# Turning two context tiles per transpose in the first expert layer, with an f32 product for the spread maxima and one-step rounding in the ternary layer

## The reference

```python
x = x + tanh(g_xattn[0]) * L0_xattn(layernorm(x), ctx)
x = x + tanh(g_ffn[0])   * L0_ffn(layernorm(x))      # 64 experts, top 6 by groups, capacity 64, plus shared
x = x + tanh(g_xattn[1]) * L1_xattn(layernorm(x), ctx)
x = x + tanh(g_ffn[1])   * L1_ffn(layernorm(x))      # ternary weights, 8-bit rounded activations
x = x + tanh(g_xattn[2]) * L2_xattn(layernorm(x), ctx)
x = x + tanh(g_ffn[2])   * L2_ffn(layernorm(x))      # 16 experts
x = x + tanh(g_xattn[3]) * L3_xattn(layernorm(x), ctx)
x = x + tanh(g_ffn[3])   * L3_ffn(layernorm(x))      # 8 experts plus shared
```

```python
# L1..L3_xattn: the same rotated context is key and value
kv_rope = kv_c * cos + rotate_half(kv_c) * sin
scores  = einsum('bhsr,bhlr->bhsl', q_r, kv_rope @ W_kr)
attn    = softmax(scores)
# L1_ffn, before each of its three matmuls
s  = 127 / clip(max(abs(x), -1), 1e-5)
qx = clip(round(x * s), -128, 127) / s
```

## Time and profile before

| | |
|---|---|
| time, median of 3 runs | 2348.73 us (2344.44 to 2351.06) |
| the profiled execution's own time | 2347.95 us |
| its span, first to last instruction | 2345.6 us |
| PE busy | 2209.3 us, 94% of the span |
| DVE, POOL, ACT busy | 1542.6, 1391.7, 1064.5 us |
| granted TensorE clock, mean | 0.958 |
| chain that ended last, share of PE | 82% |

### The profile page before, as it was taken

The page is one execution under the profiler, slowest core; times in us unless marked ns, Lnnn a source line. Parts: engine busy times, 40 slices in busy tenths (PEclk is TensorE's granted clock), DMA queues, the critical chain, the costliest instruction groups (busy, mean ns, idle before and its releaser), DMA issues.

```text
span 2345.6 us, 31158 instructions
## 1 busy us (share of the span) xinstructions
PE 2209.3 (94%) x11484; PEld 1551.9 (66%) x11484; DVE 1542.6 (66%) x2502; ACT 1064.5 (45%) x1573; POOL 1391.7 (59%) x901
## 2 busy tenths in 40 slices
PE   7789999899999997798999999989998999999988
PEld 5578888765665655565556656567886666656587
DVE  6766652478878856765878877652334788788653
ACT  4453443554555544311455555443434545555443
POOL 0352210278888874366688888824443888888744
PEclk9898999999999998799899999998999999999989
DMA  3124655211111103100121121015531111111022
GB/s 90 48 62 138 196 161 160 82 40 40 54 47 40 41 16 125 42 1 11 50 60 40 40 59 41 7 46 148 151 105 54 40 40 58 42 40 46 6 63 75
DMA packets 55394, 152.76 MB, mean 65 GB/s; under 512 B 8453, under 2 KB 14421, under 8 KB 54860
## 3 DMA queue, kind: packets, MB, share of 16 engines
q1 hardware_dynamic: 54860, 150.44, 21.3%
q10 hardware_dynamic: 384, 0.33, 0.1%
HBM read 135.88 MB, written 14.86 MB: 64 GB/s over the span
## 4 chain that ended last, share of the span: by engine, by line
PE 82%; DVE 7%; POOL 3%; ACT 2%; DMA 2%; issue 2%; SPq 0%; POOLq 0%; ACTq 0%; DVEq 0%
PE psum L890 20%; PE psum L1365 19%; PE psum L1355 10%; PE psum L1336 10%; PE psum L1357 10%; PE psum L1521 2%; PE psum L1476 2%; PE psum L1382 2%; POOL CL L1808 1%; PE psum L1250 1%; PE psum L1544 1%; PE psum L1128 1%; DMA WqrT<-in_a_WrT 1%; DMA bd<-in_blockdiag 1%; DVE mx L2333 1%
## 5 line engine op out<-in xcount | busy, mean ns | idle before, releaser
L1786 ACT ACTIVATE E<-psum 125x896 f32<-125x896 f32 x576 | 528.3, 920 | 581.1 <-PE psum L1357 554.2
L2336 DVE TENSOR_REDUCE mx<-psum 128x1 f32<-128x500 f32 x945 | 611.8, 675 | 171.9 <-PE psum L1336 170.0
L2085 POOL TENSOR_TENSOR SA<-SA,E 125x896 f32<-125x896 f32 x282 | 597.1, 2117 | 22.1
L1365 PE MATMUL psum<-E,V 125*64 125x448 f32 x2304 | 472.2, 545 | 0.0
L1355 PE MATMUL psum<-Q,K 128*125 128x448 f32 x1152 | 331.5, 369 | 2.3 <-ACT E L1786 2.3
L1336 PE MATMUL psum<-K,Q 128*128 128x500 f32 x945 | 328.7, 402 | 3.1 <-DVE Q L2274 1.9
L1357 PE MATMUL psum<-Q,K 128*125 128x448 f32 x1152 | 329.8, 367 | 0.0
L1365 PEld LDWEIGHTS psum<-E,V 125*64 125x64 f32 x2304 | 152.9, 136 | 228.6 <-issue 223.3
L2085 POOL TENSOR_TENSOR SA<-SA,SB 125x896 f32<-125x896 f32 x93 | 194.3, 2089 | 153.6 <-DVE SB L2359 153.6
L1336 PEld LDWEIGHTS psum<-K,Q 128*128 128x128 f32 x945 | 174.2, 188 | 134.1 <-issue 33.1
L1355 PEld LDWEIGHTS psum<-Q,K 128*125 128x125 f32 x1152 | 213.2, 187 | 37.1 <-ACT E L1786 6.9
(11 more groups left out here) (303 smaller groups left out, 3712.8 us busy)
## 6 DMA issues: line engine op xcount, KB each, us to landing
K<-kt_scratch SPq DMA_DIRECT2D x48, 750.0 KB, 4.9
K<-kt_scratch SPq DMA_DIRECT2D x48, 375.0 KB, 6.0
EW<-in_f_w SPq DMA_DIRECT2D x64, 256.0 KB, 6.3
kt_scratch<-kt SPq DMA_DIRECT2D x16, 750.0 KB, 4.3
WS<-in_f_w SPq DMA_DIRECT2D x31, 384.0 KB, 4.8
GB<-gates_scratch SPq DMA_DIRECT2D x36, 224.0 KB, 3.7
WoT<-in_a_WoT SPq DMA_DIRECT2D x24, 256.0 KB, 3.1
V<-in_ctx SPq DMA_DIRECT2D x16, 375.0 KB
```

The costliest lines, as they stand in the source:

```text
L1365: i = e.matmul(psum[c * DC:(c + 1) * DC, 4 + b % 2, 0:HT], V[0:LP, b, k * DC:(k + 1) * DC], E[g[n, b, k] % NE][0:LP, half[c]], start=k == ...
L1786: e.activation(E[m % NE][0:LP, :].rearrange("p (c q) -> p c q", c=2), psum[0:LP, pair:pair + 2, 0:HT], ACT.Exp).then_inc(exp_set.sem, 1)
L2085: e.tensor_tensor(SA[b % 2][0:LP, :], a[0:LP, :], x[0:LP, :], ALU.add).then_inc(sum_set.sem, 1)
L2336: e.tensor_reduce(mx[:, b % 2, j * 3 + c:j * 3 + c + 1], psum[:, bank, 0:CW], AX.X, ALU.max).then_inc(small_free.sem, 1)
```

## The change

1. A `cturn` turns six tiles by three transposes of two neighbouring tiles each (125 x 128 into 128 x 125 of PSUM). In PSUM the even tiles then stand in partitions 0 to 63 and the odd ones in 64 to 127. ACT and DVE each take them out by two instructions of 64 x 3 x 125, one for the even and one for the odd tiles, which write every second block of 125 columns of `kt`. A batch has two `cturn`s in place of three, `cadd` stands a step earlier, and the last `cturn` of a batch stands a step earlier, so that `cstore` waits for `kl_set` of turn 1 in place of turn 2.
2. `nm` becomes an f32 tile, and the `max_spread` product takes `ident` (f32); `identr` and its copy go.
3. `quantise` is one instruction: the subtraction of ROUND moves into ACT's copy out of PSUM as an immediate bias, and the minimum with 127 is left out.

```diff
-        steps += [first + [("cturn", b, 0)], [], [("cturn", b, 1)], last, [("cturn", b, 2)]]
+        steps += [first + [("cturn", b, 0)], [], last, [("cturn", b, 1)], []]
...
-    nm = mem.take("nm", [P, 2, DC], F32R)
-    identr = mem.take("ident_r", [P, P], F32R)
+    nm = mem.take("nm", [P, 2, DC], F32)
...
+    def turned_keys(b, g, odd, row):
+
+        return kt[b % 2][row:row + DC, 6 * g * LP:6 * (g + 1) * LP].rearrange("p (j k l) -> p j k l", k=2, l=LP)[:, :, odd, :]
...
-                e.wait_ge(*kl_set.at(b, 2))
+                e.wait_ge(*kl_set.at(b, 1))
...
-                e.matmul(psum[0:DC, bank, 0:P], nm[:, b % 2, :], identr[:, :], start=True, stop=True).then_inc(small_made.sem, 1)
+                e.matmul(psum[0:DC, bank, 0:P], nm[:, b % 2, :], ident[:, :], start=True, stop=True).then_inc(small_made.sem, 1)
...
-                for j in range(4):
-                    p = e.transpose(psum[0:DC, bank, j * LP:(j + 1) * LP], V[0:LP, b, (4 * g + j) * DC:(4 * g + j + 1) * DC],
+                for j in range(3):
+                    p = e.transpose(psum[:, bank, j * LP:(j + 1) * LP], V[0:LP, b, (6 * g + 2 * j) * DC:(6 * g + 2 * j + 2) * DC],
...
-                cols = slice(g * 4 * LP, (g + 1) * 4 * LP)
-                e.activation(kt[b % 2][0:DC, cols], psum[0:DC, upper_bank[f, (kind, b, g)], 0:4 * LP], ACT.Copy).then_inc(kh_set.sem, 1)
+                for odd in range(2):
+                    i = e.activation(turned_keys(b, g, odd, 0), psum[odd * DC:(odd + 1) * DC, upper_bank[f, (kind, b, g)], 0:3 * LP]
+                                     .rearrange("p (j l) -> p j l", l=LP), ACT.Copy)
+                i.then_inc(kh_set.sem, 1)
...
-                             ACT.Copy).then_inc(xqt_set.sem, 1)
+                             ACT.Copy, bias=-ROUND).then_inc(xqt_set.sem, 1)
...
-                                 ACT.Copy).then_inc(hqt_set.sem, 1)
+                                 ACT.Copy, bias=-ROUND).then_inc(hqt_set.sem, 1)
...
-        e.memset(nm[:, :, :].bitcast(F32), 0.0)
-        e.tensor_copy(identr[:, :], ident[:, :]).then_inc(*dve_own.up())
+        e.memset(nm[:, :, :], 0.0).then_inc(*dve_own.up())
...
-        e.tensor_scalar(x, x, scale, ROUND, ALU.mult, ALU.add).then_inc(*dve_own.up())
-        e.wait_ge(*dve_own.now())
-        e.tensor_scalar(x, x, ROUND, 127.0, ALU.subtract, ALU.min).then_inc(signal.sem, 1)
+
+        e.tensor_scalar(x, x, scale, ROUND, ALU.mult, ALU.add).then_inc(signal.sem, 1)
...
-                e.tensor_tensor(kt[b % 2][DC:P, cols], psum[0:DC, upper_bank[f, (kind, b, g)], 0:4 * LP],
-                                kt[b % 2][0:DC, cols].bitcast(F32), ALU.subtract).then_inc(kl_set.sem, 1)
+                for odd in range(2):
+                    i = e.tensor_tensor(turned_keys(b, g, odd, DC), psum[odd * DC:(odd + 1) * DC, upper_bank[f, (kind, b, g)], 0:3 * LP]
+                                        .rearrange("p (j l) -> p j l", l=LP), turned_keys(b, g, odd, 0).bitcast(F32), ALU.subtract)
+                i.then_inc(kl_set.sem, 1)
```

More of the change, by code:

```diff
@@ L921, in sp_fold_part @@
         if part == "fload_r" and p == 0:
-            e.wait_ge(*kl_set.at(B - 1, 2))
+            e.wait_ge(*kl_set.at(B - 1, 1))
             e.wait_ge(*v_set.at(B - 1))
```

## The result

The changed kernel took 2319.6 us (median of 4 runs, 2310.9 to 2328.1) against 2348.9 for the kernel before beside it: ratio 0.988, 95% interval 0.984 to 0.992. Measured once more, 6 runs against 23, it gave 2320.8 us against 2343.1, ratio 0.9915 (0.9893 to 0.9938). The two intervals overlap between 0.989 and 0.992. The profiled execution of after is the fastest of its four, with a span of 2309.1 us at a mean clock of 0.968.

The account below looks back on a forecast made before the run. PE was taken to bound the first expert layer and attentions, DVE the ternary layer. 2347.95 - 11.0 + 5.3 - 7.0 = 2335.2 us, set to 2335.6 towards the runs' median; range 2327 to 2342.

Parts of the forecast that it names:

- Part 1, the sum on PE: First expert layer: turns fall from 48 x 0.47 = 22.6 us to 32 x 0.35 = 11.2; 11.0 us less taken.
- The take-out: First expert layer: longer ACT and DVE copies and 0.8 us longer bank hold costed at nothing, range -2 to +4.
- The sign I had named for it: First expert layer: PE's idle time rising by over 3 us would show the take-out was mis-costed.
- the exchange of turn and addition: First expert layer: moving `cadd` a step earlier costs nothing, as it stands on DVE behind a multiplication that already waited.
- take-out becomes the bound: Rival, first expert layer: PE waits 0.8 us in each of 32 groups, losing 26 us: 2361; more than half, chance 0.04.
- few groups: Rival, first expert layer: PE waits for the take-out in some groups, ending within 0.3% (2341.7 and up); chance 0.07.
- the step that failed most: Attentions: f32 spread product's second record adds 0.11 us a batch, 48 x 0.11 = 5.3 us slower; bounds nothing to 9.6.
- free: Rival, attentions: the f32 spread product costs nothing more, as its 0.20 us already exceeds a stream; 2330.3, chance 0.12.
- the row I gave: Attentions: L1148's eight records take 0.92 us, 0.115 each, cited for the second record's price.
- Part 3: Ternary layer: DVE loses L2374, 11.2 us, of which 7.0 us reach the path; bounds 3.5 to 11.2.
- no hit any more: Ternary layer: in alternate rounds DVE's L2372 would end before POOL's product slows it; 2.6 us gained in that round.
- a forecast of 2.7: Ternary layer: two alternating rounds of h together gain 2.7 us, with two such pairs between 932 and 968 us.

Follow-up runs that it names:

- part 1 alone: Kernel before with only part 1 of the diff, the turns of two tiles with their steps: 2335.6 us, ratio 0.9972.
- e5_turns_late_add: Kernel before with only the new turns, second turn in step 2 and the addition left behind it: 2341.4 us, ratio 0.9995.
- e4_spread_wide: Kernel before with the f32 spread product, but `nm` padded to 128 columns so it takes the whole array: 2354.7 us, ratio 1.0055.
- e11_old_spread_twice: Kernel before with its fp32r spread product issued twice in a row into the same place: 2342.5 us, ratio 1.0005.
- e8_round_h: Kernel before with the one-instruction rounding for h alone, Y keeping both instructions: 2334.8 us, ratio 0.9966.
- the two filled kernels: Useless transposes put into PE's ternary-layer waits: in the kernel before 2346.8 us, ratio 1.0014; in the changed kernel with turns moved 2317.5 us, 0.9895.
- e7_turns_twice: Kernel before with only the new turns, each group's three transposes issued twice: 2343.2 us, ratio 1.0002.
- e9_turns_moved: Changed kernel with turns that would stand just ahead of down products put a step later: 2318.9 us, ratio 0.9899 to the kernel before.

## Why the prediction was wrong, point by point

**Part 1, the sum on PE: right.** 10.6 us less busy PE at equal clock, 11.0 forecast. **The take-out: mis-sized.** "I take nothing, with -2 to +4": PE's idle time in the stage grows by 4.2 us in part 1 alone and by 5.6 and 5.9 in the changed kernel. The waiting line is L1516, the matching rows, which takes the bank of a turn. A bank is now held for two ACT instructions of 0.48 us and two of DVE of 0.55, 2.05 us in place of 1.25, as I had said. My reason for pricing it at nothing failed: with a third of the turns gone, I argued, a bank's last user lies further back. At the places that matter it lies as near as before, with two down products and one matching-rows task between (at pair 14 after, 1.5 us of PE work from 281.64 us on), and there are five of them where there were four. The sign I had named for it, PE's idle time up by over 3 us, is there. -11.0 + 4.2 is -6.8, and the run of part 1 alone gave -6.6, within 2.1 to 10.8; that the two agree so closely is luck. `e5_turns_late_add` shows that the longer take-out by itself can eat all of the gain, and that the exchange of turn and addition, which I had costed at nothing, saved 5.4 us of it. The rival "take-out becomes the bound" had the right mechanism; 5 waits of 1 us each are its "few groups".

**Part 2: the step that failed most.** "The second record has to stream the 128 columns again ... 48 x 0.11 = 5.3 us", and "I take 5.3, since the attentions have no PE gap to hide it in". The second record is there, 0.11 us behind the first. But I had not asked what the old product cost beyond its stream. In the earlier trace rows it has 0.20 us in the chain, nearly twice the 0.11 of a stream in the earlier trace rows; I named this only as a word in favour of "free" and bounded the term from below by nothing, so a gain lay outside my bounds. The fp32r product, 64 columns wide as it is, stops both halves. Pairs of values products follow each other at 0.375 us. The product begins 0.10 later than a pair would, the values start 0.20 behind it, and the next pair takes 0.05 more: 0.35 in all. The f32 product costs 0.23 (0.35 less 0.12): two streams on one half, beside the other half's values. The 0.12 a batch is what the distances of the batches show. `e4_spread_wide` shows that the f32 product loses this at full width, `e11_old_spread_twice` that the stop, and not the product, was what one paid for. Measured -6.1 for a forecast of +5.3 us: the term is 11 us off. The price of 0.11 for the second record came out, but not from the row I gave: L1148 streams 64 columns, not 128. In the trace of before records that stream 4 columns behind a load of 128 columns also start 0.112 us apart, so it is not the stream that sets the 0.115 of that row.

The Trainium skill, page "TensorEngine Tiling (Array Packing)", section "Performance Considerations", lets a stationary side of 64 columns or fewer be tiled two-fold by columns. By that rule both the old and the new product would leave half of the array free; the timeline agrees for f32 and not for fp32r, whose 128x64 product stops both halves.

**Part 3: right in size, in part by luck.** 7.0 us forecast, 6.3 measured alone (1.9 to 10.8). DVE's timeline of after, the rounding of h in the middle rounds, for the earlier trace rows:

```profile
910.42 0.75 DVE L2377 TENSOR_SCALAR h<-h,h_scale 128x1024 f32<-128x1024 f32 x1
916.61 2.51 DVE L2377 TENSOR_SCALAR h<-h,h_scale 128x1024 f32<-128x1024 f32 x1
924.39 2.60 DVE L2377 TENSOR_SCALAR h<-h,h_scale 128x1024 f32<-128x1024 f32 x1
932.32 0.75 DVE L2377 TENSOR_SCALAR h<-h,h_scale 128x1024 f32<-128x1024 f32 x1
939.58 2.20 DVE L2377 TENSOR_SCALAR h<-h,h_scale 128x1024 f32<-128x1024 f32 x1
```

and PE's turns of h in the same rounds, for the earlier trace rows:

```profile
911.51 1.04 PE L1602 MATMUL psum<-ident,h 128*128 128x128 f32 x8
...
919.26 1.06 PE L1602 MATMUL psum<-ident,h 128*128 128x128 f32 x8 [1.88 <-DVE h L2377]
...
927.14 1.06 PE L1602 MATMUL psum<-ident,h 128*128 128x128 f32 x8 [1.88 <-DVE h L2377]
...
934.55 1.04 PE L1602 MATMUL psum<-ident,h 128*128 128x128 f32 x8
```

My reason "no hit any more" did not come true: three of seven roundings still take 2.2 to 2.6 us beside POOL's product. What is gained is that a round pays one instruction less, hit or not: two hit rounds take 7.8 and 7.9 us, where 9.1 and 8.6 alternated. The pair is 15.6 for 17.7, 2.1 us for a forecast of 2.7; the first round, not hit at all, takes 5.2 for 8.0. From the first to the last turn it is 50.5 us before, 44.6 and 43.9 with the rounding alone, 41.6 and 41.2 in the changed kernel. Of the last 3 us, 2 stand in the first round (7.2 with the rounding alone, 5.2 in the changed kernel; see the last section). No run shows that parts 1 or 2 set it, and `e8_round_h` has a round of 5.2 without them. So the sum came out though the rounds do not go as I had said. PE's clock rises in the layer as well, but the two filled kernels speak against it as the cause.

**The sum.** In ratios of 2341.75: forecast -11.0 + 5.3 - 7.0 = -12.7; measured -6.6 - 6.1 - 6.3 = -19.0. Two errors of opposite sign, 4.4 us too good (the take-out) and 11.4 too bad (the spread product), and one term about right. They explain 6.3 us of the miss, not all 16 between 2335.6 and 2319.6. The rest is that the first measurement gave 29 us and the second 20 to 22. Its four runs had a higher clock (0.961 to 0.968, mean 0.964) than the six of the second (mean 0.9615); by the 0.44 above, an estimate, that is worth 4 to 5 us. As the two intervals overlap, chance alone can make the difference, and its cause stays open.

## What to carry to other kernels

A product that stands between column-tiled products is paid by what it stops, not by its own stream: read the distance from the last product ahead of it to the first behind, and compare with the distance without it. When work is shortened on a PE-bound stretch, the order of the list around it decides how much arrives: look up for each task which task held its PSUM bank before, and what PE does in between. Where two down products and one more task are all that lies between, 0.8 us more of take-out cost about 1 us a place here. Exchanging one turn and one addition in the list was worth 5.4 us. And compare stages of two profiles only at equal granted clock: 17.7 us between two executions of one kernel went with the clock alone.

## What the runs showed of the hardware

- An fp32r product of 128x64 leaves no half of the array to others and costs 0.35 us amid f32 products of 64 columns; a second one right behind it costs 0.05 to 0.08. The f32 product of the same shape, with two records, costs 0.23 there, and one of 128x128 costs 0.57.
- A load of 128 columns was hidden behind a turn of 125 columns: 96 transposes more took 7 us, 0.07 each, in `e7_turns_twice`. Where the stream is short it shows: records of 4 columns behind such loads start 0.112 us apart in the kernel before.
- DVE's 128x1024 rounding beside POOL's product was not slowed where it began 0.05 us or more ahead (`e9_turns_moved`, 919.74 and 919.79: 0.75 us). It was slowed where POOL's had begun, or both began within 0.01 us. DVE's began at 910.42 and POOL's at 910.51 in the changed kernel: 0.75 us for DVE, and 2.89 for POOL's in place of 2.35. With the rounding alone DVE's began at 928.84 and POOL's at 928.85: 2.90 for DVE, 2.34 for POOL's. The round took 5.2 us in the one and 7.2 in the other.
- PE's clock in one stage of one kernel came out between 0.89 and 0.97 in two executions, with the same work and waits.
